# Shared norm statistics in the gated node pass, the tails' product first on TensorE, and the last layer's edgeless blocks at three in eight steps

## The chip, the cores and the metric

The kernel runs on one core of a Trainium2 chip. The metric is the device time of one execution in microseconds, where less is better. The engines of a core are PE (TensorE, its weight loads shown apart as PEld), DVE (VectorE), ACT (ScalarE), POOL (GpSimd) and SP (SyncE, which only issues DMAs here). Each runs its own instruction stream, and they meet at semaphores.

## The reference

Four graph networks follow one another over 100,000 nodes of 128 features and 50,000 edges sorted by target (`dst`); a layernorm of `x + f(x)` follows each. The first is two graph convolutions, the second a gated one with two norms, the third attention with three heads, the fourth six graph convolutions (widths 64, 32, 16, 32, 64, 128) and a last product. What matters here, cut down:

```python
def _layernorm(x, axis=-1, eps=1e-05):
    m = jnp.mean(x, axis=axis, keepdims=True)
    v = jnp.var(x, axis=axis, keepdims=True)
    return (x - m) / jnp.sqrt(v + eps)

# second network, behind the edges' messages (agg) and their batch norm
h = agg + x
mu = h.mean(axis=-1, keepdims=True); var = h.var(axis=-1, keepdims=True)
h = (h - mu) * jax.lax.rsqrt(var + EPS) * ln_gamma + ln_beta
h = jax.nn.relu(h)
return h + x                       # and then the second norm, _layernorm

# fourth network
def _gcn_conv(h, W, b, row, col, norm, n):
    h = h @ W
    msg = h[row] * norm[:, None]
    return jax.ops.segment_sum(msg, col, num_segments=n) + b
h = relu(_gcn_conv(x, W1, b1, ...)) ... h = relu(_gcn_conv(h, W6, b6, ...))
return h @ Wf + bf
```

## The kernel before

The nodes are kept in two regions. Region a has a row for each edge slot that ends a run of equal targets: 99 blocks (`NBA`) of 512 rows, 4 rows to a partition. Region b has all nodes without the edges' part: 98 blocks (`NB`) of 1024 rows, 8 rows to a partition. A pass is one `nc.Block` that ends in a barrier of all engines (`end_pass`). Inside it each engine runs a list of stages `(fn, lag, blocks)` through `pipeline`: at step t it calls, in the order of the list, each `fn` for block t - lag. So the order of a list is the order of the engine's instructions within a step, and nothing is sorted at run time. A fourth entry `every` spaces the blocks of a stage by that many steps.

**The gated node pass** (`gated_node_pass`, class `GatedNode`, tiles `cn_*`) runs the second network's node part for a and b side by side. In a step DVE does, in this order: copies of the scores, `stats_1` for a and b (`bn_stats` and `bn_aggr` on `v`), `factors_2` for a and b (minus the mean, the reciprocal of the root, their product), `shift`, `rectify`, `stats_2` for a and b (on `y`), `factors_1` for a and b. ACT does `root_2`, `normalise_1`, `root_1`, `normalise_2` and `evacuate`, each for a and then b. POOL does `gain` and `batch_norm`. Class `Norm` (L597 to L642) holds the tiles and the instructions of one norm of one region: four `Norm` objects are in use, two for a, two for b.

**The graph passes** g1 to g8 (`graph_pass`) are one convolution each. POOL gathers 4 tiles of 128 source rows per step (L1318) into one of 4 buffers; it may refill a buffer once DVE has combined the block that used it. DVE adds the rows up run by run (`add_up`, L880 and L884), in `combine`. At the last step, block 98, `join` (L896 to L902) copies the unfinished last run of each partition (`last`), waits until PE has multiplied it with `link_up` (`sum_tails`, L892), and adds the result. On PE `sum_tails` stands behind the products of that step.

With the edge part of one layer, a pass also carries layers for region b that need no edges, as `others`: tuples of a lag, `every`, the layer it follows and the layer (tiles `g_bb_*` for the first of them, `g_bc_*` for the last layer's). The last layer, the costliest (W6, Wf, bias, residual, norm), is split over g5, g6 and g7: `last_layer(0)` to `(2)` with 33, 33 and 32 blocks, one every 3 steps, from step 5 in g5 and from step 0 in g6 and g7. Within it (`deep`) PE does `turn` at lag 0, `multiply_turned` at 2 and `multiply_b` at 4; ACT `evacuate` at 1, `evacuate_b` at 3, `root` at 6, `normalise` at 8; DVE `last_rows` and `variance` at 5 and `factors` at 7. `turn` of a block waits until `evacuate_b` of the block before it has emptied the PSUM tile `p_t`.

## Time and profile before

| | us |
|---|---|
| median of 3 runs (12212.0 to 12260.14) | 12238.38 |
| profiled execution, whole | 12327.15 |
| its span | 12325.4 |
| gated node pass in it | 4090 to 5313 |
| g3, g4 | 7611 to 8319, 8319 to 8928 |
| g5 | 8928 to 9743 |
| g6 | 9743 to 10401 |
| g7 | 10401 to 11062 |
| g8 | 11062 to 12325 |

| engine | busy us | share of the span |
|---|---|---|
| PE | 6734.9 | 55% |
| DVE | 8163.0 | 66% |
| ACT | 5969.5 | 48% |
| POOL | 7335.5 | 60% |

The passes lie end to end, so a microsecond won in one is a microsecond of the whole. The shares of the whole span are means over passes with different limits; each pass has to be read for itself. The profiled execution took 0.7% longer than the median of the other runs.

### The profile page before, as it was taken

Reading aid. Unit: us, or ns where it says so; the run is one execution under the profiler, and the core shown is the slowest. Engines: PE = TensorE matmul, PEld = TensorE weight load, DVE = VectorE, ACT = ScalarE, POOL = GpSimd, SP = SyncE. Lnnn points to the kernel's source line nnn. Section 1 sums busy time; section 2 is a strip of 40 time slices with the busy share of each in tenths; the row PEclk is TensorE's granted clock in tenths of the full one; section 3 lists DMA queues with packets and bytes.
Section 4 is the critical chain, followed back from the end, with each engine's and each line's share of the span. In section 5 each row is a group of like instructions: output and inputs, shape, how many; then the busy total and the mean of one; then the engine's idle time right before and its main releaser. Section 6 shows DMA issues by size and latency. Waiting matters only on the chain. (4 is left out here: it accounts for less than half of the span.)

```text
span 12325.4 us, 143095 instructions
## 1 busy us (share of the span) xinstructions
PE 6734.9 (55%) x32436; PEld 5466.4 (44%) x32436; DVE 8163.0 (66%) x34473; ACT 5969.5 (48%) x14065; POOL 7335.5 (60%) x6801
## 2 busy tenths in 40 slices
PE   2141666665766465677746665773455565554443
PEld 1021555654555455567745665662233333332222
DVE  1063778995666899989988886444555565664444
ACT  0000445775666899989957775331123332322222
POOL 5701446886777688866636665546554455556665
PEclk6575888887888555578868887555566655665555
DMA  3238777883222577734424443443333332332221
GB/s 95 91 119 264 235 237 257 289 289 117 70 70 70 171 220 220 217 126 140 142 90 161 162 165 128 135 130 76 83 107 115 100 90 87 105 103 56 56 58 53
DMA packets 1019506, 1694.53 MB, mean 137 GB/s; under 512 B 304877, under 2 KB 535080, under 8 KB 1018594
## 3 DMA queue, kind: packets, MB, share of 16 engines
q1 hardware_dynamic: 782752, 1361.06, 33.0%
q0 software_dynamic: 175936, 218.82, 7.9%
q10 hardware_dynamic: 59970, 105.49, 2.6%
q8 instruction: 270, 4.42, 0.1%
q14 instruction: 578, 4.73, 0.1%
HBM read 988.03 MB, written 707.78 MB: 138 GB/s over the span
## 5 line engine op out<-in xcount | busy, mean ns | idle before, releaser
L1318 POOL DMA_INDIRECT g_got<-scaled,row_src x2352 | 2230.9, 949 | 1754.8 <-issue 681.8
L588 PE MATMUL g_a_p_z<-sb_L_gnn_W,g_a_u_t 128*128 128x128 f32 (+3 forms) x2574 | 665.7, 403 | 1163.7 <-ACT g_a_u_t L1163 439.5
L1163 ACT COPY g_a_u_t<-g_a_p_t 128x512 f32<-128x512 f32 (+3 forms) x495 | 226.2, 457 | 1800.4 <-remote 1223.5
L880 DVE SCALAR_TENSOR_TENSOR g_sums<-g_got,first,g_sums 128x128 f32<-128x128 f32 (+3 forms) x3136 | 869.9, 277 | 344.2 <-DMA g_got<-scaled,row_src 113.2
L588 PEld LDWEIGHTS g_a_p_z<-sb_L_gnn_W,g_a_u_t 128*128 128x128 f32 (+1 forms) x2574 | 491.6, 270 | 1342.4 <-issue 606.8
L588 PE MATMUL g_bb_p_z<-sb_L_gnn_W,g_bb_u_t 128*128 128x128 f32 (+2 forms) x4302 | 842.9, 363 | 308.9 <-DVE g_bb_z L1055 280.6
L884 DVE SCALAR_TENSOR_TENSOR g_sums<-g_sums,cont,g_got 128x128 f32<-128x128 f32 (+3 forms) x3128 | 887.6, 284 | 90.8 <-DVE g_sums L880 65.9
L1318 POOL DMA_INDIRECT g_got<-xs,idx_src x392 | 370.7, 946 | 934.5 <-POOLq L174 552.9
L588 PEld LDWEIGHTS g_bb_p_z<-sb_L_gnn_W,g_bb_u_t 128*128 128x128 f32 x4302 | 752.7, 260 | 369.9 <-ACT g_bb_u_t L1163 261.0
L1163 ACT COPY g_bb_u_t<-g_bb_p_t 128x1024 f32<-128x1024 f32 (+2 forms) x294 | 233.6, 795 | 1318.8 <-remote 555.1
L1230 POOL DMA_INDIRECT out<-g_a_o,idx_out x396 | 395.3, 998 | 361.3 <-ACT g_a_o L640 234.6
L579 PE MATMUL g_bb_p_t<-ident,g_bb_own 128*128 128x128 f32 x2151 | 365.1, 311 | 430.5 <-DMA g_bb_own<-in_x 390.2
L2383 POOL DMA_INDIRECT gb_got<-x,row_src x392 | 393.7, 1004 | 242.2 <-POOLq L174 138.3
L1475 POOL DMA_INDIRECT cg_got_src<-x,row_src x392 | 399.8, 1020 | 228.5 <-issue 101.3
L1055 DVE TENSOR_TENSOR g_bb_z<-g_bb_p_z,row_L_gnn_b 128x1024 f32<-128x1024 f32 (+1 forms) x196 | 186.6, 952 | 508.1 <-remote 383.0
L1524 PE MATMUL cg_p_g<-gate_w,cg_t_d 128*128 128x259 f32 x784 | 313.3, 488 | 380.8 <-ACT cg_t_a L1548 314.3
L579 PEld LDWEIGHTS g_bb_p_t<-ident,g_bb_own 128*128 128x128 f32 x2151 | 302.4, 168 | 461.9 <-DMA g_bb_own<-in_x 391.8
L1137 PE MATMUL g_a_p_t<-g_a_u_t,sb_L_gnn_W 64*128 64x512 f32 x198 | 200.7, 1114 | 557.9 <-ACT g_a_u_t L1163 325.8
L2507 PE MATMUL gb_p_m<-head_w,gb_u_t 128*128 128x128 f32 x2376 | 409.9, 350 | 149.8 <-DVE gb_a_r L2479 115.4
L1475 POOL DMA_INDIRECT cg_got_dst<-x,row_dst x392 | 418.7, 1068 | 119.5 <-issue 119.5
L790 PE MATMUL p_hist<-f_hot_lo,f_hot_hi 128*98 128x512 bf16 x784 | 228.4, 451 | 474.0 <-issue 414.9
L1191 ACT ACTIVATE g_bb_o<-g_bb_z 128x1024 f32<-128x1024 f32 (+3 forms) x294 | 196.6, 669 | 596.3 <-DVE g_bb_z L1055 355.3
(500 smaller groups left out, 24621.7 us busy)
## 6 DMA issues: line engine op xcount, KB each, us to landing
raw<-gb_u SPq DMA_DIRECT2D x98, 768.0 KB
xs<-f_o ACTq DMA_DIRECT2D x97, 516.0 KB
f_x<-in_x ACTq DMA_DIRECT2D x97, 512.0 KB
g_bb_own<-in_x SPq DMA_DIRECT2D x97, 512.0 KB
wide<-g_bb_o SPq DMA_DIRECT2D x97, 512.0 KB
g_bb_own<-wide SPq DMA_DIRECT2D x97, 512.0 KB
g_bb_res<-in_x SPq DMA_DIRECT2D x97, 512.0 KB
x<-g_bb_o SPq DMA_DIRECT2D x97, 512.0 KB
```

Source lines behind the costliest of these rows:

```text
L579: last = nc.tensor.transpose(dst_psum[0:n * k, q * P:q * P + p], tile[0:p, q * g * k:(q * g + n) * k], ident[0:p, 0:p])
L588: last = nc.tensor.matmul(dst_psum[0:p, q * g * width:(q * g + n) * width], turned_tile[0:n * k, q * P:q * P + p], weight[0:n * k, 0:n * w ...
L790: ins = nc.tensor.matmul(p_hist[0:HI, h * half:(h + 1) * half], hot_hi[b.s][:, (2 * c + h) * HI:(2 * c + h + 1) * HI], hot_lo[b.s][:, c * ...
L880: nc.vector.scalar_tensor_tensor(out=self.firsts, in0=new, scalar=first[:, col], in1=self.firsts, op0=ALU.mult, op1=ALU.add).then_inc(run_ ...
L884: nc.vector.scalar_tensor_tensor(out=self.part(b.s, c), in0=before, scalar=cont[:, col], in1=new, op0=ALU.mult, op1=ALU.add).then_inc(run_ ...
L1163: last = nc.scalar.copy(to, source)
L1230: nc.gpsimd.indirect_dma_start(self.to, bass.IndirectOffsetOnAxis(ap=idx_out[:, b.n * CH + c:b.n * CH + c + 1], axis=0), self.o_s[b.s4][:, ...
L1318: pool.indirect_dma_start(got[b.s4][:, c * row:(c + 1) * row], None, table, bass.IndirectOffsetOnAxis(ap=index[:, b.n * CH + c:b.n * CH + ...
L1475: pool.indirect_dma_start(got[b.s4][:, c * D:(c + 1) * D], None, x1, bass.IndirectOffsetOnAxis(ap=index[:, b.n * CH + c:b.n * CH + c + 1], ...
L1524: last = nc.tensor.matmul(p_g[c][:, :], rows, weight, start=(i == 0), stop=(i == 2))
L2383: pool.indirect_dma_start(got[b.s4][:, c * D:(c + 1) * D], None, x2, bass.IndirectOffsetOnAxis(ap=row_src[:, b.n * CH + c:b.n * CH + c + 1 ...
L2507: last = nc.tensor.matmul(p_m[:, c * D:(c + 1) * D], u_t[h][:, c * P:(c + 1) * P], head_w[:, h * D:(h + 1) * D], start=(h == 0), stop=(h = ...
```

## The change

Three things change.

1. In the gated node pass a class `BothNorms` takes the place of the four `Norm` objects: one object for each norm, with tiles 12 columns wide (4 of a, then 8 of b). The statistics still take one `bn_stats` and one `bn_aggr` for each of the 12 rows, but all 12 `bn_stats` come first and all `bn_aggr` behind them, with one wait between. Root, minus mean, reciprocal and product are one instruction each for both regions. Each such instruction waits for both regions. The scaling on ACT stays one instruction per row.
2. On PE `sum_tails` moves to the head of the list in all graph passes but g5 (`plain`).
3. The spacing of blocks becomes a pair `(steps, blocks)`: block n comes n * steps // blocks steps behind the lag. The last layer runs at (8, 3), which gives gaps of 2, 3 and 3 steps, with 32, 33 and 33 blocks in g5, g6 and g7. Its `evacuate_b` moves from lag 3 to lag 2, the step in which its input is multiplied. All others stay at one block a step.

```diff
 def pipeline(eng, stages):
-    stages = [(fn, lag, blocks, every[0] if every else 1) for fn, lag, blocks, *every in stages]
-    for t in range(max(lag + (blocks - 1) * every + 1 for _, lag, blocks, every in stages)):
-        for fn, lag, blocks, every in stages:
-            n, off = divmod(t - lag, every)
-            if off == 0 and 0 <= n < blocks:
-                fn(Block(n // UNROLL, n % UNROLL, n == blocks - 1))
+    stages = [(fn, {lag + n * every[0][0] // every[0][1] if every else lag + n: n for n in range(blocks)}, blocks)
+              for fn, lag, blocks, *every in stages]
+    for t in range(max(max(at) + 1 for _, at, _ in stages)):
+        for fn, at, blocks in stages:
+            if t in at:
+                fn(Block(at[t] // UNROLL, at[t] % UNROLL, at[t] == blocks - 1))
...
-                    return self.on(lag, every, (self.normalise, 8), (self.evacuate_b, 3), (self.root, 6), (self.evacuate, 1)), []
+                    return self.on(lag, every, (self.normalise, 8), (self.evacuate_b, 2), (self.root, 6), (self.evacuate, 1)), []
...
-                        stages = []
+                        stages = [] if plain else in_a((edges.sum_tails, 0))
...
-                        stages += in_a((edges.sum_tails, 0))
-                        if not plain:
-                            stages += in_a((na.turn, 0))
+                        stages += in_a((edges.sum_tails if plain else na.turn, 0))
...
+            class BothNorms:
...
+                def variance(self, b, tiles):
+                    stats, mv = self.stats[b.s], self.mv[b.s]
+                    self.steps.at(b)
+                    for (first, p, j), tile in zip(self.rows(b), tiles):
+                        for q in range(j):
+                            last = nc.vector.bn_stats(stats[0:p, 6 * (first + q):6 * (first + q + 1)],
+                                                      tile[0:p, q * D:(q + 1) * D])
+                    last.then_inc(self.steps.sem, 1)
+                    nc.vector.wait_ge(self.steps.sem, self.steps.count())
+                    for first, p, j in self.rows(b):
+                        for q in range(first, first + j):
+                            last = nc.vector.bn_aggr(mv[0:p, 2 * q:2 * q + 2], stats[0:p, 6 * q:6 * q + 6])
+                    last.then_inc(self.varied, 1)
...
+                def factors(self, b):
+                    self.factor_step.at(b)
+                    nc.vector.wait_ge(self.rooted, b.n + 1)
+                    nc.vector.tensor_scalar(self.minus[b.s], self.mv[b.s][:, 0:2 * self.G:2], -1.0, None, ALU.mult)
+                    nc.vector.reciprocal(self.rstd[b.s][:, :], self.sd[b.s][:, :]).then_inc(self.factor_step.sem, 1)
+                    nc.vector.wait_ge(self.factor_step.sem, self.factor_step.count())
+                    nc.vector.tensor_tensor(self.nmr[b.s][:, :], self.rstd[b.s][:, :], self.minus[b.s], ALU.mult
+                                            ).then_inc(self.factored, 1)
...
+                        def stats_1(b):
+                            dve.wait_ge(mark_a.combined, b.n + 1)
+                            dve.wait_ge(mark_b.combined, min(b.n + 1, NB))
+                            n1.variance(b, [n.v_s[b.n % 3] for n in (na, nb)])
...
+                        pipeline(dve, [(na.scores, 9, NBA), (nb.scores, 9, NB), (stats_1, 2, NBA), (factors_2, 6, NBA),
                                        (na.shift, 5, NBA), (nb.shift, 5, NB), (na.rectify, 5, NBA), (nb.rectify, 5, NB),
-                                       (na.stats_2, 5, NBA), (nb.stats_2, 5, NB), (na.factors_1, 2, NBA),
-                                       (nb.factors_1, 2, NB)])
+                                       (stats_2, 5, NBA), (factors_1, 2, NBA)])
...
+                        pipeline(act, [(n2.root, 6, NBA), (na.normalise_1, 3, NBA), (nb.normalise_1, 3, NB), (n1.root, 2, NBA),
+                                       (na.normalise_2, 6, NBA), (nb.normalise_2, 6, NB), (na.evacuate, 7, NBA),
+                                       (nb.evacuate, 7, NB)])
...
-        third = -(-NB // 3)
+        EACH, LAST = (1, 1), (8, 3)
+        thirds = [NB * part // 3 for part in range(4)]
```

**DVE in the gated node pass**, from the first statistics of a step to its second norm's factors. `cn_a_v` and `cn_b_v` are the inputs of the first norm, `mv` mean and variance, `sd` the root, `rstd` and `nmr` the factors. Before:

```order
L611 BN_STATS cn_a_n_stats<-cn_a_v 128x6 x4
L615 BN_AGGR cn_a_n_mv<-cn_a_n_stats 128x2 x4
L611 BN_STATS cn_b_n_stats<-cn_b_v 128x6 x8
L615 BN_AGGR cn_b_n_mv<-cn_b_n_stats 128x2 x8
L628 TENSOR_SCALAR cn_consts<-cn_a_n_mv 128x4
L629 RECIPROCAL cn_a_n_rstd<-cn_a_n_sd 128x4
L632 TENSOR_TENSOR cn_a_n_nmr<-cn_a_n_rstd,cn_consts 128x4
L628 TENSOR_SCALAR cn_consts<-cn_b_n_mv 128x8
L629 RECIPROCAL cn_b_n_rstd<-cn_b_n_sd 128x8
L632 TENSOR_TENSOR cn_b_n_nmr<-cn_b_n_rstd,cn_consts 128x8
```

After:

```order
L1706 BN_STATS cn_n_stats<-cn_a_v 128x6 x4
L1706 BN_STATS cn_n_stats<-cn_b_v 128x6 x8
L1712 BN_AGGR cn_n_mv<-cn_n_stats 128x2 x12
L1723 TENSOR_SCALAR cn_consts<-cn_n_mv 128x12
L1724 RECIPROCAL cn_n_rstd<-cn_n_sd 128x12
L1726 TENSOR_TENSOR cn_n_nmr<-cn_n_rstd,cn_consts 128x12
```

Six factor instructions of 4 and 8 columns become three of 12, and the eight statistics of b stand ahead of the aggregation of a.

**PE at the last host step of g3**, with the tails' product at L892 (L893 after). Before:

```order
L588 MATMUL g_a_p_z<-sb_L_gnn_W,g_a_u_t 128x64 x2
L588 MATMUL g_bb_p_z<-sb_L_gnn_W,g_bb_u_t 112x64 x3
L588 MATMUL g_bc_p_z<-sb_L_gnn_W,g_bc_u_t 128x64 x2
L579 MATMUL g_bc_p_t<-ident,g_bc_own 128x128 x2
L892 MATMUL g_sums<-g_last,link_up 128x64
L579 MATMUL g_a_p_t<-ident,g_a_z 128x128 x2
```

After:

```order
L893 MATMUL g_sums<-g_last,link_up 128x64
L589 MATMUL g_a_p_z<-sb_L_gnn_W,g_a_u_t 128x64 x2
L589 MATMUL g_bb_p_z<-sb_L_gnn_W,g_bb_u_t 112x64 x3
L589 MATMUL g_bc_p_z<-sb_L_gnn_W,g_bc_u_t 128x64 x2
L580 MATMUL g_bc_p_t<-ident,g_bc_own 128x128 x2
```

The tails' product moves ahead of the products of a, b and the second edgeless layer.

**PE in the middle of g5**, where `g_bc_p_t` is written by `turn` (64x128 x8) and by `multiply_turned` (128x512 x2), and `g_bb` is the layer with one block a step. Before:

```order
L1115 MATMUL g_bc_p_t<-ident,g_bc_own 64x128 x8
L588 MATMUL g_bb_p_z<-sb_L_gnn_W,g_bb_u_t 128x256 x2
L579 MATMUL g_bb_p_t<-ident,g_bb_own 128x128 x2
L588 MATMUL g_bc_p_z<-sb_L_gnn_Wf,g_bc_h_t 128x128 x8
L588 MATMUL g_bb_p_z<-sb_L_gnn_W,g_bb_u_t 128x256 x2
L579 MATMUL g_bb_p_t<-ident,g_bb_own 128x128 x2
L1137 MATMUL g_bc_p_t<-g_bc_u_t,sb_L_gnn_W 128x512 x2
L588 MATMUL g_bb_p_z<-sb_L_gnn_W,g_bb_u_t 128x256 x2
L579 MATMUL g_bb_p_t<-ident,g_bb_own 128x128 x2
L1115 MATMUL g_bc_p_t<-ident,g_bc_own 64x128 x8
```

After:

```order
L580 MATMUL g_bb_p_t<-ident,g_bb_own 128x128 x2
L1138 MATMUL g_bc_p_t<-g_bc_u_t,sb_L_gnn_W 128x512 x2
L1116 MATMUL g_bc_p_t<-ident,g_bc_own 64x128 x8
L589 MATMUL g_bb_p_z<-sb_L_gnn_W,g_bb_u_t 128x256 x2
L580 MATMUL g_bb_p_t<-ident,g_bb_own 128x128 x2
L589 MATMUL g_bb_p_z<-sb_L_gnn_W,g_bb_u_t 128x256 x2
L580 MATMUL g_bb_p_t<-ident,g_bb_own 128x128 x2
L589 MATMUL g_bc_p_z<-sb_L_gnn_Wf,g_bc_h_t 128x128 x8
L1138 MATMUL g_bc_p_t<-g_bc_u_t,sb_L_gnn_W 128x512 x2
```

In a gap of two steps `turn` of the next block now follows `multiply_turned` directly, where before the two were never in one step.

## Rows read from the trace of the kernel before

**Rows 1.** Busy time by stretch: us, then PE, PEld, DVE, ACT, POOL; clock, DMA, GB/s.
```profile
4090.00:5313.00 1223.00, 718.54 (x3530) 682.61 (x3530) 1159.52 (x6687) 1144.31 (x2947) 953.82 (x592) 0.53 0.70 214
8928.00:9743.00 815.00, 419.74 (x1514) 297.71 (x1514) 449.71 (x2142) 264.33 (x559) 370.75 (x392) 0.64 0.37 113
9743.00:10401.00 658.00, 390.90 (x1223) 247.77 (x1223) 397.51 (x2043) 198.41 (x462) 370.75 (x392) 0.56 0.30 86
```

**Rows 2.** Waits, 4500 to 4800 (gated node pass): total us, times, longest.
```profile
ACT cn_b_n_sd L620 <- DVE cn_b_n_mv L615: 10.5, 25, 0.7
```

**Rows 3.** DVE in order of time in that pass: start, us, line; last, one group's span.
```profile
4602.56 0.86 DVE L611 BATCH_NORM_STATS2 cn_a_n_stats<-cn_a_v 128x6 f32<-128x128 f32 x4
4603.45 0.38 DVE L615 BATCH_NORM_AGGREGATE cn_a_n_mv<-cn_a_n_stats 128x2 f32<-128x6 f32 x4
4603.75 1.61 DVE L611 BATCH_NORM_STATS2 cn_b_n_stats<-cn_b_v 128x6 f32<-128x128 f32 x8
4605.39 0.64 DVE L615 BATCH_NORM_AGGREGATE cn_b_n_mv<-cn_b_n_stats 128x2 f32<-128x6 f32 x8
4605.95 0.15 DVE L628 TENSOR_SCALAR cn_consts<-cn_a_n_mv 128x4 f32<-128x4 f32 x1
...
4606.28 0.17 DVE L628 TENSOR_SCALAR cn_consts<-cn_b_n_mv 128x8 f32<-128x8 f32 x1
...
4606.67 0.70 DVE L1794 TENSOR_TENSOR cn_a_p_h<-cn_a_y,cn_consts 128x512 f32<-128x512 f32 x1
...
4609.00 1.22 DVE L1802 SCALAR_TENSOR_TENSOR cn_b_y<-cn_b_p_h,cn_b_x_r 128x1024 f32<-128x1024 f32 x1
4610.14 0.86 DVE L611 BATCH_NORM_STATS2 cn_a_n_stats<-cn_a_y 128x6 f32<-128x128 f32 x4
...
L611 DVE BATCH_NORM_STATS2 cn_a_n_stats<-cn_a_v x396: 274/279/296, 4098.0 to 5267.3; 128x6 f32<-128x128 f32 x198
```

**Rows 4.** ACT in order of time, the same steps.
```profile
4606.25 0.28 ACT L620 ACTIVATE cn_a_n_sd<-cn_a_n_mv,eps 128x4 f32<-128x4 f32 x1
4606.44 0.29 ACT L620 ACTIVATE cn_b_n_sd<-cn_b_n_mv,eps 128x8 f32<-128x8 f32 x1
...
4612.63 0.30 ACT L620 ACTIVATE cn_a_n_sd<-cn_a_n_mv,cn_eps 128x4 f32<-128x4 f32 x1
```

**Rows 5.** Waits for the tails' product: all eight passes, then DVE in g3 and g6.
```profile
  PE g_sums L892: 22.6, 8
...
8302.13 0.22 DVE L898 COPY g_joined<-g_sums 128x64 f32<-128x64 f32 x1 [7.71 <-PE g_sums L892]
...
10377.51 0.17 DVE L898 COPY g_joined<-g_sums 128x16 f32<-128x16 f32 x1 [4.67 <-PE g_sums L892]
```

**Rows 6.** Waits of POOL in g5 (8930 to 9712), then g6 (9745 to 10377).
```profile
POOL g_got L1318 <- DVE g_sums L1015: 277.7, 30, 9.8
...
POOL g_got L1318 <- DVE g_a_own L1018: 137.2, 34, 5.7
```

**Rows 7.** DVE in g5, in order of time: a block of the last layer; the stall after.
```profile
9302.32 1.22 DVE L1067 TENSOR_TENSOR g_bc_y<-g_bc_p_z,g_bc_res 128x1024 f32<-128x1024 f32 x1
...
9307.07 0.20 DVE L880 SCALAR_TENSOR_TENSOR g_sums<-g_got,first,g_sums 128x16 f32<-128x16 f32 x1
...
9325.99 0.69 DVE L1055 TENSOR_TENSOR g_bb_z<-g_bb_p_z,row_L_gnn_b 128x512 f32<-128x512 f32 x1 [9.00 <-remote]
```

**Rows 8.** DVE at the ends of g5 and g6: last host rows, next pass.
```profile
9714.78 0.23 DVE L1091 SCALAR_TENSOR_TENSOR g_a_o<-g_sums,inv 128x64 f32<-128x64 f32 x1
...
9742.81 0.29 DVE L866 COPY g_sums<-row_L_gnn_bf 128x128 f32<-128x128 f32 x1 [7.51 <-PEq L174]
...
10385.31 0.29 DVE L1091 SCALAR_TENSOR_TENSOR g_a_o<-g_sums,inv 128x128 f32<-128x128 f32 x1
...
10401.30 0.29 DVE L866 COPY g_sums<-row_L_gnn_bf 128x128 f32<-128x128 f32 x1 [7.51 <-PEq L174]
```

**Rows 9.** PE in the tail of g5, in order of time.
```profile
9719.76 1.89 PE L1115 MATMUL g_bc_p_t<-ident,g_bc_own 128*64 128x128 f32 x8 [1.30 <-ACT g_bc_h_t L1176]
```

More of the change, by code:

```diff
@@ L1680, in gated_node_pass, with __init__ @@
             class GatedNode:
-                def __init__(self, sb, ps, r, consts, p_sc, other):
+                def __init__(self, sb, ps, r, beta, p_sc, norms, other):
                     n, G = r.name, r.per
@@ L1697, in __init__ @@
                     self.x_t = sb(f"{n}_x_t", [D, G * P])
-                    self.n1, self.n2 = Norm(sb, f"{n}_n1", r), Norm(sb, f"{n}_n2", r)
+                    (self.n1, self.n2), self.first = norms, 0 if self.a else rows_a.per
                     self.p_x = ps(f"{n}_p_x", [P, G * P])
@@ L1804, in rectify @@
                         in1=self.x_r[b.s][0:p, 0:j * D], op0=ALU.max, op1=ALU.add).then_inc(m.summed_b, 1)
-                def stats_2(self, b):
-                    nc.vector.wait_ge(self.m.summed_b, b.n + 1)
-                    self.n2.variance(self.link_c, self.y_s[b.n % 4], b, self.m.varied_b)
-                def factors_2(self, b):
-                    m = self.m
-                    self.link_g.at(b)
-                    nc.vector.wait_ge(m.rooted_b, b.n + 1)
-                    if b.after(2):
-                        nc.vector.wait_ge(m.normed_b, b.n - 1)
-                    self.n2.factors(self.link_g, b, m.factored_b, minus=self.minus[1][b.s])
                 def scores(self, b):
@@ L1851, in normalise_2 @@
                         act.wait_ge(m.turned, b.n - 1)
[L1852 removed]
+                    self.n2.scale(self.o_s[b.s], self.y_s[b.n % 4], b, self.first, p, j).then_inc(m.normed_b, 1)
                 def evacuate(self, b):
@@ L2539, in build @@
         attention_pass()
-        third = -(-NB // 3)
+        EACH, LAST = (1, 1), (8, 3)
+        thirds = [NB * part // 3 for part in range(4)]
         def last_layer(part):
-            start = part * third
-            return layer(mark_c, 64, D, scaled2[64], NA, out, w["L3_gnn_W6"], None, True, to_base=0, start=start,
-                         blocks=min(third, NB - start), residual=x3, residual_base=NA, last_w=w["L3_gnn_Wf"],
+            return layer(mark_c, 64, D, scaled2[64], NA, out, w["L3_gnn_W6"], None, True, to_base=0, start=thirds[part],
+                         blocks=thirds[part + 1] - thirds[part], residual=x3, residual_base=NA, last_w=w["L3_gnn_Wf"],
                          last_bias=brow["L3_gnn_bf"], bias_col=bcol["L3_gnn_b6"])
```

114 lines of the change are left out of this document (71 added, 43 removed).

## The prediction

> **What bounds the kernel now.** I read the stretches of the passes first, since they lie end to end. In the gated node pass DVE is busy 1160 of 1223 us and ACT 1144, while g5 takes 815 us and g6 658, both with no engine busy over 61% of them [rows 1]. So the first is bound by throughput and the graph passes by waits.
>
> In the gated node pass I then read who waits. ACT waits for DVE's last `bn_aggr` on b once a step, 10.5 us over 25 steps or 0.42 us a step [rows 2]. DVE waits for nobody: its instructions follow one another without a gap of note [rows 3]. DVE sets the step, with ACT 0.42 us behind it. The first statistics of 99 blocks start between 4098.0 and 5267.3 [rows 3]: (5267.3 - 4098.0) / 98 = 11.93 us a step.
>
> In g5 to g7 POOL gathers for 3 steps on end and then waits until DVE has freed a buffer. In g5 that wait is 277.7 us in 30 times, 9.3 us each; in g6 137.2 us in 34 times, 4.0 us each [rows 6]. During the wait DVE stands still too, for 9.00 us before 9325.99 [rows 7], until PE's products are announced to it. After that DVE does a block of the last layer, from 9302.32 to 9307.07 in the cycle before [rows 7], and only then frees a buffer. So 4.75 us of each g5 wait is the last layer's `last_rows` and `variance`, which stand ahead of `combine` in this pass; in g6 they stand behind it.
>
> **Part 1, shared norm factors and statistics: -77 us.** Per step, on DVE:
> - Factors. The three instructions of a take 4606.28 - 4605.95 = 0.33 us, those of b 4606.67 - 4606.28 = 0.39 [rows 3]. From 4 to 8 columns it grew by 0.06, so 12 columns take 0.45. The pair costs 0.72, so 0.27 goes; two norms: 0.54.
> - Statistics. Four `bn_stats` take 4603.45 - 4602.56 = 0.89, eight take 5.39 - 3.75 = 1.64; four `bn_aggr` 0.30, eight 0.56 (to 5.95) [rows 3]. On the same lines 12 take 2.39 and 0.82, 3.21 in all for 3.39 now: 0.18 for each norm, 0.36.
> - A new wait. `stats_2` of a starts at 4610.14 while `rectify` of b, from 9.00 for 1.22 us, runs until 10.22 [rows 3]. Now it waits for that end and a handoff of 0.03 (a's aggregation starts 3.45, its statistics end 3.42): 0.11 lost. `stats_1` waits for b's input as well, which POOL made a step earlier by the lags (batch norm 1, statistics 2): nothing.
> The sum is 0.54 + 0.36 - 0.11 = 0.79 us, times 98 = 77 us.
>
> ACT must follow. Its work is 11.93 - 0.42 = 11.51 us a step. It loses one root of `root_1`, 4606.44 - 4606.25 = 0.19, and one of `root_2`, 0.30 [rows 4], and comes to 11.02; DVE comes to 11.14. ACT stays just behind, so the cap of this part is (11.93 - 11.02) x 98 = 89 us. ACT's `normalise_2` of a now needs the factors of both regions; in the step shown those of b are done at 4606.67, about when ACT reaches it (4606.44 + 0.19), and the shared ones come 0.4 us earlier relative to that, so it does not wait. Behind DVE and ACT stand PE and POOL: POOL is busy 954 of 1223 us and PE 719 [rows 1], so both have slack.
>
> A rule speaks for more. That rows 3 start b's first factor 0.33 us after a's, though the three instructions last 0.15 to 0.17 us each behind one another, shows starts that overlap earlier instructions. The Trainium skill ("VectorE: DVE Perf Modes", § The DRAIN you can't avoid) says that the next DVE instruction does not start until the pipe is empty. By it each of the 6 removed instructions would give back its whole duration, about 1 us a step, and ACT's cap of 89 us would be reached. In rows 3 the rule does not hold for these short instructions, so the sum goes by the starts.
>
> **Part 2, the tails' product first: -8 us outside g5 to g7.** DVE waited 22.6 us for it in 8 passes, 7.71 of them in g3 [rows 5]. In g6 it was 4.67 [rows 5]; I put g5 (unchanged) and g7 at some 3 together, so that about 15 are in the other five. The copy of 0.17 us [rows 5], a product and the way back remain, which I put at 0.6 in each, so 12 can go. PE must still do the products that stood ahead, and edgeless layers end g3 and g4 later than the join: I take two thirds. Ends: 0 and -12.
>
> **Part 3, three blocks in eight steps: -29 us, less 8.** A pass has 99 steps. At every 3 the last of 33 blocks starts at 5 + 96 = 101 in g5 and is scaled 8 steps later, at 109; at (8, 3) the last of 32 starts at 5 + 82 = 87 and is stored by step 96. The tails go:
> - g5: from region a's last rows, 9714.78, to the next pass, 9742.81, is 28 us [rows 8]. A store and the barrier remain, some 7: -21. But 32 blocks instead of 30 now have `last_rows` inside the host steps, each for a wait of 9.3 instead of about 4.0 [rows 6]: +11. Net -10.
> - g6: 10385.31 to 10401.30 is 16.0 us, and shrinks by 9; the join wait shrinks by 4; the block that DVE does between join and last rows (4.75 as above) is gone; one block more inside costs 1 to 3. Net -15.
> - g7: the same with a shorter tail, estimated from g6's rows: the join wait, smaller there, 1.5; a block's DVE work, which in part lies beside the tail already, 4; an extra block +1.5. Net -4.
>
> **The price of the gaps of two.** There `turn` of a block stands behind `multiply_turned` of the block before, and waits for ACT's `evacuate_b` in the same step. The tail of g5 has just this sequence today: PE idles 1.30 us for it [rows 9]. It will do so at 11 places in each of three passes: 33 x 1.30 = 43 us of PE time. If POOL's gathers hide it, 0; if it is all on the path, 43. PE is idle about half of g5 and 40% of g6 [rows 1], and one place in a burst of three steps seldom decides: I take +8. The phase of the blocks against the bursts of three steps changes too, in either direction (rivals 1 and 3).
>
> **Sum.** -77 - 8 - 29 + 8 = -106 us against the profiled span of 12325.4. The execution around it adds 2 us and doesn't change; the median of the runs is 0.7% below it, and I apply the same difference to it: 12238 - 106 = **12132 us**, 0.87% less. What a measurement of this kernel can tell from no change is about 0.5%, 61 us.
>
> **Rivals.**
> 1. *The last layer comes loose from the bursts in g5.* Every 3 steps and bursts of 3 steps lock: its 4.75 us always fall between PE's announcement and the freed buffer [rows 7]. At 2, 3, 3 they drift; two thirds would fall where POOL still gathers: 32 x 4.75 x 2/3 = 101, of which some 70 remain after other waits. Against it: a late `combine` stops POOL by itself, and the burst then locks to the new place. 12062 us. Chance 0.13.
> 2. *The joined waits take back half of part 1.* If DVE finds region b's input not ready at `stats_1`, or ACT the shared factors, 0.4 us a step go: +39, 12171 us. Against it: the slack of a whole step on POOL. Chance 0.10.
> 3. *The gaps of two lie on the path, and the shifted phases cost g6 and g7 a little.* +43 for all places instead of +8, and about +15 for phases: 12182 us. Chance 0.15.
> 4. *Slower: PE stalls for a whole burst at the gaps of two.* PE's products of 9314 to 9318 reached DVE only at 9326, after 9.00 us idle [rows 7]. If the step's new round trip from PE to ACT and back meets this delay each time, `turn` waits 9 us at 33 places: +297 on the sum, 12429 us. It decides from (106 + 61) / 33 = 5 us a place for a slowdown of over 0.5%. Against it: the delay passes together for all products of a burst. Chance 0.04.
> 5. *DVE gives back whole durations* (the rule above: what the removed instructions last, 6 x about 0.16), and ACT caps it at 89: 12120 us. Chance 0.05.
> That the change does less than it says has no case: the order shows three factor instructions for six and the tail empty of the last layer.
>
> **How the numbers follow.** The forecast, 12132, has 0.53; its own range is 12090 to 12175, from the caps of part 1 (60 to 89), part 2 (0 to 12) and the gaps (0 to 43). The range for 8 in 10 leaves out rival 4, half of rival 1 and a third of rival 3: 12050 to 12205. Faster by over 0.5% means under 12177: the forecast but for 0.05, rivals 1 and 5, 0.06 of rival 2 and 0.05 of rival 3, in all 0.77. Slower by over 0.5% is rival 4: 0.04. The rest, 0.19, is within.
>
> **What would show it.** The gated node pass 77 us shorter (1146 instead of 1223), DVE still busy 94% or more of it and ACT still waiting for DVE's `bn_aggr`, now below 0.2 us a step; if POOL's v is waited for by DVE, rival 2. The waits for the tails' product down to some 5 us in all. No last-layer instruction after region a's last rows in g5 to g7, and the starts of the next passes 10, 15 and 4 us earlier against their own starts. POOL's waits in g5 at 9 us, about 32 of them; if they fall below 240 us in sum, rival 1. PE waiting for `g_bc_h_t` 1.3 us at 11 places in a pass; at 5 us or more, rival 4. Wrong altogether would be a gated node pass that keeps its 11.9 us a step.

## The result and the profile after

| | before | after |
|---|---|---|
| median of the timed runs, us | 12229.0 | 12030.7 |
| profiled execution's span, us | 12325.4 | 12030.4 |
| gated node pass | 1226.9 | 1157.6 |
| g1, g2 | 790.8, 921.8 | 777.9, 921.4 |
| g3, g4 | 707.9, 608.8 | 682.1, 599.4 |
| g5 | 815.1 | 730.6 |
| g6, g7 | 658.5, 660.9 | 611.4, 635.3 |
| g8 | 1263.3 | 1263.2 |

The changed kernel takes 0.9836 of the time before (95% interval 0.9824 to 0.9847): 198 us less, where 106 were forecast and the range ended at 12050. The two profiles lie 295 us apart, since that of before was slower than its timed runs and that of after was not. So some rows above show more than the change did. In the gated edge pass, whose code is the same, 1222.7 became 1209.7; and g3, of which the change touches only the place of the tails' product, took 682 to 720 us in the twelve profiles of this case whose whole lasts over 12000 us (the others come from chips that run every version faster, see the experiments). The median before is over four runs now, where the forecast had three and 12238. Of the runs below one, at 13940 us beside five from 10484 to 10497, was in a slower state of the chip and isn't counted.

**Gated node pass.** The windows of the trace after (us, then busy time of PE, PEld, DVE, ACT, POOL, clock, DMA share, GB/s), for the gated node pass, g5 and g6, as in [rows 1]:

```profile
4062.00:5220.00 1158.00, 715.72 (x3534) 689.76 (x3534) 1089.97 (x6106) 1101.80 (x2751) 950.49 (x592) 0.53 0.73 225
8789.00:9520.00 731.00, 378.22 (x1486) 261.35 (x1486) 446.77 (x2122) 257.25 (x548) 369.71 (x392) 0.71 0.42 124
9520.00:10131.00 611.00, 358.76 (x1223) 237.22 (x1223) 403.94 (x2043) 198.17 (x462) 369.79 (x392) 0.58 0.33 93
```

The waits of ACT and POOL in 300 us of it, as in [rows 2] (total, times, longest):

```profile
POOL cn_b_y L1824 <- ACT cn_b_y L1731: 39.3, 26, 1.8
...
ACT cn_n_sd L1717 <- DVE cn_n_mv L1712: 0.7, 2, 0.4
```

DVE in order of time in one step, as in [rows 3], and last the group of the first statistics:

```profile
4592.09 0.86 DVE L1706 BATCH_NORM_STATS2 cn_n_stats<-cn_a_v 128x6 f32<-128x128 f32 x4
4592.87 1.62 DVE L1706 BATCH_NORM_STATS2 cn_n_stats<-cn_b_v 128x6 f32<-128x128 f32 x8
4594.52 0.91 DVE L1712 BATCH_NORM_AGGREGATE cn_n_mv<-cn_n_stats 128x2 f32<-128x6 f32 x12
4595.35 0.16 DVE L1723 TENSOR_SCALAR cn_consts<-cn_n_mv 128x12 f32<-128x12 f32 x1
4595.40 0.22 DVE L1724 RECIPROCAL cn_n_rstd<-cn_n_sd 128x12 f32<-128x12 f32 x1
...
4595.73 0.69 DVE L1833 TENSOR_TENSOR cn_a_p_h<-cn_a_y,cn_consts 128x512 f32<-128x512 f32 x1
...
4598.07 1.21 DVE L1841 SCALAR_TENSOR_TENSOR cn_b_y<-cn_b_p_h,cn_b_x_r 128x1024 f32<-128x1024 f32 x1
4599.38 0.87 DVE L1706 BATCH_NORM_STATS2 cn_n_stats<-cn_a_y 128x6 f32<-128x128 f32 x4
...
4601.83 0.91 DVE L1712 BATCH_NORM_AGGREGATE cn_n_mv<-cn_n_stats 128x2 f32<-128x6 f32 x12
...
4603.40 0.86 DVE L1706 BATCH_NORM_STATS2 cn_n_stats<-cn_a_v 128x6 f32<-128x128 f32 x4
...
L1706 DVE BATCH_NORM_STATS2 cn_n_stats<-cn_a_v x396: 272/275/295, 4072.9 to 5169.8; 128x6 f32<-128x128 f32 x198
```

The step is (5169.8 - 4072.9) / 98 = 11.19 us, where it was 11.93. A statistics block takes 4595.35 - 4592.09 = 3.26 us (3.39 before), the factors 4595.73 - 4595.35 = 0.38 (0.72 for the pair). The new wait is there: `rectify` of b ends at 4598.07 + 1.21 = 4599.28, and the statistics behind it start at 4599.38. From start to start that is 1.31 us, where it was 4610.14 - 4609.00 = 1.14. ACT hardly waits for the statistics now: 0.7 us in all, where it was 10.5. In these 300 us ACT is busy 296.9 and DVE 293.1, so the two are level, and by that more taken from DVE alone would hardly shorten the step.

**Ends of the passes.** The waits for the tails' product in all eight passes, as in [rows 5], and DVE at the end of g5, as in [rows 8]:

```profile
  PE g_sums L893: 8.8, 8
...
9515.96 0.17 DVE L899 COPY g_joined<-g_sums 128x16 f32<-128x16 f32 x1 [0.70 <-PE g_sums L893]
...
9517.42 0.23 DVE L1092 SCALAR_TENSOR_TENSOR g_a_o<-g_sums,inv 128x64 f32<-128x64 f32 x1
9520.62 0.30 DVE L867 COPY g_sums<-row_L_gnn_bf 128x128 f32<-128x128 f32 x1 [2.97 <-PEq L175]
```

From region a's last output to the next pass it is now 3.2 us (9517.42 to 9520.62); it was 28. From the join (`g_joined`) to the next pass it is 4.7 us (9515.96 to 9520.62), where it was 29.5 (9713.33 to 9742.81).

**POOL in g5 and g6**, its waits for a free buffer, as in [rows 6] (total, times, longest), and then PE's greatest wait in g5:

```profile
POOL g_got L1319 <- DVE g_sums L1016: 235.0, 35, 9.6
...
POOL g_got L1319 <- DVE g_a_own L1019: 116.5, 36, 5.5
...
PE g_bc_p_t L1116 <- ACT g_bc_h_t L1177: 201.8, 20, 11.7
```

In g5 the wait is 42.7 us shorter, though PE now stands 201.8 us for ACT's `g_bc_h_t` (64.9 before), which rival 4 feared. POOL in order of time, with its idle time before each burst in brackets, shows where it is won:

```profile
9239.27 0.94 POOL L1319 DMA_INDIRECT g_got<-scaled,row_src  x1 [9.52 <-DVE g_sums L1016]
...
9248.01 0.94 POOL L1319 DMA_INDIRECT g_got<-scaled,row_src  x1 [0.30 <-issue]
9252.17 0.94 POOL L1319 DMA_INDIRECT g_got<-scaled,row_src  x1 [3.22 <-DVE g_sums L1016]
...
9265.91 0.94 POOL L1319 DMA_INDIRECT g_got<-scaled,row_src  x1 [0.30 <-issue]
9276.23 0.94 POOL L1319 DMA_INDIRECT g_got<-scaled,row_src  x1 [9.38 <-DVE g_sums L1016]
```

Each row is a gather, 1.25 us apart within a burst. From 9239.27 there are 8 of them (two steps), then 3.22 us of idle time; from 9252.17 there are 12 (three steps), then 9.38. So a gap of two steps between blocks of the last layer makes a cycle of 9252.17 - 9239.27 = 12.9 us, and a gap of three one of 24.1. Two thirds of the cycle before, 24.24 us for three steps, would be 16.2 for two: each gap of two gives back 3.3 us. The last layer's block on DVE (4.75 us) lies in another place in the two cycles: in the trace before it is wholly inside a pause of POOL for 28 of 33 blocks and behind the last gather for the other 5; in the trace after it is wholly inside a pause for 20 of 32, partly for one, and beside a burst for 11, one in three.

**What holds the pauses.** PE in g5 of the kernel before, and DVE's first row that needs its product:

```profile
9314.71 1.03 PE L588 MATMUL g_bb_p_z<-sb_L_gnn_W,g_bb_u_t 128*128 128x256 f32 x4
...
9315.58 0.38 PE L579 MATMUL g_bb_p_t<-ident,g_bb_own 128*128 128x128 f32 x2
9315.89 0.29 PEld L1137 LDWEIGHTS g_bc_p_t<-g_bc_u_t,sb_L_gnn_W 64*128 64x128 f32 x2 [0.17 <-issue]
...
9325.99 0.69 DVE L1055 TENSOR_TENSOR g_bb_z<-g_bb_p_z,row_L_gnn_b 128x512 f32<-128x512 f32 x1 [9.00 <-remote]
```

By the records PE ends the product for `g_bb_z` at 9315.74; DVE gets it at 9325.99, 2.5 us after POOL's burst, whose last gather ended at 9323.51. The ends of PE's rows are a model: the Trainium skill ("Perfetto Trace Analysis", § Tensor Engine Instruction (MATMUL, LD_WEIGHTS)) says that the profiler estimates them and that the update of the semaphore comes when PSUM acknowledges the write. So the rows don't tell whether the product itself was late or only its announcement; that it reached DVE 10.25 us behind the modelled end is measured.

The same place on a chip of another kind (see the experiments), where DVE starts 0.17 us behind PE's end while POOL gathers on:

```profile
8099.37 1.49 PE L589 MATMUL g_bb_p_z<-sb_L_gnn_W,g_bb_u_t 128*128 128x256 f32 x3
...
8100.97 0.94 POOL L1319 DMA_INDIRECT g_got<-scaled,row_src  x1 [0.30 <-issue]
8101.03 0.68 DVE L1056 TENSOR_TENSOR g_bb_z<-g_bb_p_z,row_L_gnn_b 128x512 f32<-128x512 f32 x1
...
8102.21 0.94 POOL L1319 DMA_INDIRECT g_got<-scaled,row_src  x1 [0.30 <-issue]
```

### The profile page after: what moved, and what is told of

The parts are those of the page before. It is cut to its first block and busy times, and to the rows that moved or that the text cites. A ratio compares the mean times of both kernels' runs of the same rounds, so it can differ in the third digit from the quotient of the medians.

```text
span 12030.4 us, 142319 instructions
## 1 busy us (share of the span) xinstructions
PE 6638.5 (55%) x32436; PEld 5450.5 (45%) x32436; DVE 8099.9 (67%) x33889; ACT 5912.3 (49%) x13869; POOL 7313.3 (61%) x6801
## 5 line engine op out<-in xcount | busy, mean ns | idle before, releaser
L2565 PEld LDWEIGHTS gb_p_m<-head_w,gb_u_t 128*128 128x128 f32 x2376 | 406.9, 269 | 162.8 <-issue 153.0
L694 POOL DMA_INDIRECT f_got<-in_x,idx_dst x396 | 399.9, 1010 | 128.2 <-issue 128.2
```

The lines of the kernel that those rows point to most:

```text
L694: pool.indirect_dma_start(got[b.s4][:, c * D:(c + 1) * D], None, a["x"], bass.IndirectOffsetOnAxis(ap=idx_dst[:, b.n * CH + c:b.n * CH + c ...
L2565: last = nc.tensor.matmul(p_m[:, c * D:(c + 1) * D], u_t[h][:, c * P:(c + 1) * P], head_w[:, h * D:(h + 1) * D], start=(h == 0), stop=(h = ...
```

## The experiments

The runs fell on six chips (the number of the first result's isn't recorded), of two kinds. On chips 3, 4, 11 and 15, as on the chip of the first result, the kernel before takes 12229 to 12316 us, and products that PE finishes late in a burst of POOL's gathers reach the other engines only behind the burst: I call this the hold. On chips 7 and 12 it takes 10518 and 10524, and there is no hold: in g5 of the four profiles there DVE waits 62 times for the product of `g_bb_z`, and starts 0.04 us behind PE's end each time. In g5 of the kernel before, with the hold, 30 of 31 such starts come more than 1 us behind it, at the median 9.3. Not every product is held there. Of the waits of DVE and ACT for region b's products in the bursts of 12, 31 end within 0.5 us of PE's end, all but one of them for products that PE ended in the first 6.2 us of a burst; 56 end 8.0 to 10.3 us behind it, for products ended 6.9 us or more after a burst's start. The two kinds differ in the first pass too, which has none of the changed code: PE's waits in 578 us of it, before, and then without the hold:

```profile
PE p_hist L790 <- issue: 414.9, 24, 19.1
...
PE p_hist L791 <- DVE f_hot_lo L725: 14.3, 3, 13.9
```

Every run is compared with the kernel before on its own chip.

**1. The norms alone** (without the hold, chip 12): the changed kernel with the other two parts taken back.

```diff
-                    return self.on(lag, every, (self.normalise, 8), (self.evacuate_b, 2), (self.root, 6), (self.evacuate, 1)), []
+                    return self.on(lag, every, (self.normalise, 8), (self.evacuate_b, 3), (self.root, 6), (self.evacuate, 1)), []
...
-                        stages = [] if plain else in_a((edges.sum_tails, 0))
+                        stages = []
...
-                        stages += in_a((edges.sum_tails if plain else na.turn, 0))
+                        stages += in_a((edges.sum_tails, 0))
+                        if not plain:
+                            stages += in_a((na.turn, 0))
...
-        EACH, LAST = (1, 1), (8, 3)
-        thirds = [NB * part // 3 for part in range(4)]
+        EACH, LAST = (1, 1), (3, 1)
+        thirds = [0, 33, 66, NB]
```

> Only the shared statistics and factors of the gated node pass; all else is as in the kernel before. If the gated node pass of the changed kernel (1157.6 us, before 1226.9) owes its time to this part alone, the pass takes 1157 us again and the whole is 65 to 75 us faster than the kernel before (ratio about 0.994), with g5 at 815 us, g6 at 658 and g7 at 661. Rival: the profile of before was slow by chance in this pass too, and the part alone is worth under 50 us in the timed runs.

0.9934 (0.9921 to 0.9946), 72 us; the gated node pass 1155.0 us. The pass owes its time to this part, and it is as long with the hold, where it was 1154 to 1158 us in all profiles with this code. The expected times of g5 to g7 were missed, since this chip has no hold: 529.9, 522.6 and 511.9 us.

**2 and 3. The tails' product alone** (chip 12, then chip 4 with the hold). The edit is the kernel before with `sum_tails` at the head of PE's list.

> Only the tails' product at the head of PE's list in all graph passes but g5. Theory A, the part acts at the join alone: waits for the product fall from 22.6 to about 9 us, g3 is some 7 us shorter than 708, the whole 8 to 13 us faster. Theory B, the 20 us by which the gathers of g3 ran shorter in the changed kernel belong to it: g3 takes 682 us here too, and the whole is 35 us or more faster.

> The tails' product first, alone, again. With the hold: 10 to 20 us, since in the first two traces its waits fell by 14 us; the 20 us of g3's gathers are chance, because g3 alone varied between 682 and 720 us in five profiles with the same work. Rival: it is worth over 30 us there. Without the hold: 9 us as before.

Without the hold 0.9990 (0.9981 to 0.9999), 9 us. With it 0.9997 (0.9986 to 1.0009): nothing that can be told from zero. The 10 to 20 us that I expected there did not come, though the waits for the product fell from 22.6 us to some 9. g3 took 704.4 us, so the short g3 of the first profile is not this part's work (it is 682.4 on chip 11 as well, and 695.7 to 720.1 on the others with the hold). What the waits gave up is in part paid back by the products that now stand behind: from the join to the next pass g3 went from 16.8 to 18.3 us.

**4 and 5. The spacing alone** (chip 12, then chip 4). The edit is the kernel before with `(8, 3)`, the new thirds and `evacuate_b` at lag 2.

> Only the last layer at three blocks in eight steps, with its second evacuation a step earlier; gated node pass and tails' product as before. Theory A, the gain of g5 is the spacing of the blocks: POOL's gathers come in bursts of 12 behind a gap of three steps (cycle 24.1 us) and of 8 behind a gap of two (12.6 us), g5 takes 730 us, g6 about 616, g7 about 638, the whole 125 to 150 us faster in the profile. In the timed runs, whose sum was 198, what is left after norms (70) and tails (10) is about 120. Theory B, part of it belongs to the other edits: g5 stays above 760 us.

> The last layer's spacing alone, again, for a chip that holds PE's announcements while POOL gathers (the kernel before takes about 12250 us there). With the hold: the whole 198 less the norms' 72 and the tails' 9 are its own, 110 to 125 us (ratio about 0.9905), of which g5's gathers are 30 to 45, g6's and g7's 35 or less, the tails of the passes 49, the join waits behind a burst 25. If it gives under 60 us, the parts help each other and the sum of them taken alone is short of the whole. Without the hold: 36 us as before.

Without the hold 0.9965 (0.9952 to 0.9978), 36 us, far from the 120 of theory A, which was made for bursts and pauses that this chip doesn't have; with it 0.9909 (0.9888 to 0.9929), 105 us by the medians and 112 by the ratio, as expected. POOL's waits for a buffer in g5, by the spacing of three without the hold (norms alone), by the new spacing without it, and by the new spacing with it:

```profile
POOL g_got L1319 <- DVE g_sums L1016: 0.3, 1, 0.3
...
POOL g_got L1319 <- DVE g_sums L1016: 23.3, 20, 2.1
...
POOL g_got L1319 <- DVE g_sums L1016: 242.1, 35, 9.7
```

Without the hold POOL hardly waits, and the gaps of two cost: the gathers of g5 take 505.8 us from first to last instead of 488.1. With the hold they gain: 720.1 instead of 755.8 (chip 4, tails' product alone).

**6. The changed kernel again** (chip 3, with the hold).

> The changed kernel once more, unaltered. If this chip holds PE's announcements while POOL gathers (the kernel before then takes about 12230 us), it repeats the first result: ratio 0.984, g5 at 730 us. If it doesn't (the kernel before takes about 10520 us), the parts measured apart add up: 72 + 9 + 36 = 117 us, a ratio of 0.989, with g5 at 522 us and g6 at 501. A sum over 135 or under 100 would say that the parts act on each other.

0.9847 (0.9827 to 0.9867), 180 us. The parts alone come to 72 + 1 + 105 to 112 = 178 to 185 (the 72 from a chip without the hold): they add up. Its passes lie between those of the two first profiles: g5 744.6, g6 638.2, g7 640.6. Without the hold the whole was not run; the parts alone sum to 117.

**7. g5 at every three steps, 30 blocks** (chip 3).

```diff
-        thirds = [NB * part // 3 for part in range(4)]
+        thirds = [0, 30, 64, NB]
...
-                           (5, LAST, mark_b, last_layer(0))))
+                           (5, (3, 1), mark_b, last_layer(0))))
```

> The changed kernel with g5's blocks at every three steps again, 30 of them so that none stands in the tail, and 34 each in g6 and g7. Theory A (a gap of two steps costs where gathers are bound by nothing else, and gains where announcements are held): without the hold g5's gathers take 488 us instead of the 506 of the spacing of eight, and the kernel is 10 to 18 us faster than the changed one; with the hold they take about 757 - 10 instead of 713, and it is about 35 us slower. Theory B (the spacing of the blocks doesn't matter, only where they end): within 5 us of the changed kernel on either chip.

0.9899 (0.9874 to 0.9924), 49 us slower than the changed kernel on the same chip, and g5 is 49 us longer: 793.7 us against 744.6. Its gathers take 756.8 us, as before the change, against 726.7. The last gather to the join takes 26.6 against 12.6, since the pass ends on a burst of three steps. So the spacing itself is worth some 30 us in the gathers, which the forecast left out of its sum. The earlier `evacuate_b` is in this kernel too, so by itself it gives g5 nothing; whether the gaps of two need it was not run.

**8. The wait for ACT at every block** (chip 3, one run).

```diff
-                    return self.on(lag, every, (self.multiply_b, 4), (self.multiply_turned, 2), (self.turn, 0))
+                    return self.on(lag, every, (self.multiply_b, 4), (self.multiply_turned, 3), (self.turn, 0))
...
-                    return self.on(lag, every, (self.normalise, 8), (self.evacuate_b, 2), (self.root, 6), (self.evacuate, 1)), []
+                    return self.on(lag, every, (self.normalise, 8), (self.evacuate_b, 3), (self.root, 6), (self.evacuate, 1)), []
...
-        EACH, LAST = (1, 1), (8, 3)
-        thirds = [NB * part // 3 for part in range(4)]
+        EACH, LAST = (1, 1), (3, 1)
+        thirds = [0, 33, 66, NB]
```

> The changed kernel with the last layer at every three steps in all three passes (33, 33, 32 blocks) and its first product and second evacuation at lag 3, so that the next block's transposes stand right behind the product and wait for ACT at every block. Theory A, this wait itself is what costs: without the hold g5's gathers take over 500 us, 1 us or more for each of 30 blocks above 488; with the hold bursts are cut as behind a gap of two (8 gathers and fewer). Theory B, the wait is hidden and only the two steps' distance is short: without the hold 488 us; with it bursts of 12 and cycles of 24.1 us.

POOL's waits in g5, then in g6:

```profile
POOL g_got L1319 <- DVE g_sums L1016: 277.1, 31, 9.7
...
POOL g_got L1319 <- DVE g_a_own L1019: 289.9, 32, 10.2
```

In g5 nothing changed: 277.1 us, bursts of 12, as theory B had it. But PE waited for ACT only 42.1 us here, 32 times, 1.3 us each, and not the 10 us that it waits at the gaps of two. So the run shows that a short wait at every block doesn't cut a burst; what a long one would do behind a gap of three it doesn't tell. In g6 POOL's waits went from 137.2 to 289.9 us, the pass took 822.6 us where it was 658.5, and g7 went from 661 to 742; the one execution took 12490 us, 182 more than the kernel before. In g6 DVE's last rows now wait 209.0 us for their product (108.4 before), which reaches them in the pause, 17.1 us after the burst's start. Of the two moves in this kernel it isn't told apart which does it.

**9 and 10. g5 at every two steps** (chip 7 without the hold, chip 4 with it).

```diff
-                           (5, LAST, mark_b, last_layer(0))))
+                           (5, (2, 1), mark_b, last_layer(0))))
```

> The changed kernel with the last layer's 32 blocks in g5 one every two steps, from step 5 to 67, and none behind. Where PE's announcements are held during POOL's gathers, as in the first two traces, theory A (a gap of two steps cuts the burst to 8 gathers, and its last rows lie beside the burst) expects cycles of 12.6 us for two steps up to step 70 and about 24 us for four steps behind it: g5 at about 640 us instead of 730.6. Theory B (the 4.7 us of every block lie on the path, wherever they are) expects no less than 730. Where nothing is held, as in the three runs before this one, g5 is bound by the gathers and stays at 515 to 530 us by both.

> The changed kernel with g5's 32 blocks one every two steps, again. With the hold, theory A (a gap of two steps gives bursts of 8 gathers and 12.6 to 13.0 us for two steps, whatever stands beside it): 32 such cycles, then four steps in about 24 us: g5 at 620 to 650 us instead of 731 to 745, the whole 90 to 110 us faster than the changed kernel. Theory B (the cheap short cycle was paid for by the two long ones around it, 24.1 us each): nothing below 720. Without the hold: 600 us against 522, as before.

Without the hold g5 takes 599.6 us, where 515 to 530 were expected, and the kernel 10486 beside 10518 (one run each). With it g5 takes 658.2, and the kernel 12050, 0.9788 (0.9768 to 0.9807), by the ratios 73 us less than the changed kernel; g5 at 620 to 650 and 90 to 110 us were expected. POOL's waits in g5, first without the hold, then with it:

```profile
POOL g_got L1319 <- DVE g_sums L1016: 107.7, 29, 7.8
...
POOL g_got L1319 <- DVE g_sums L1016: 163.8, 42, 14.2
```

With the hold the cycles are 12.6 to 16.0 us, most of them 13 to 14, so theory A holds, and its price of 12.6 to 13.0 was a little low. Without it two steps take over 12 us as well, against 10 that the gathers need: 64 steps cost 100 us. The short cycle is nearly the same on both kinds of chip. It gains only where the alternative is worse. On chip 4 the short bursts leave most of the hold behind them, too: only 3 of DVE's 29 waits for the product of `g_bb_z` end more than 1 us behind PE's end.

**11. One buffer less for POOL** (chip 4).

```diff
-                                pool.wait_ge(mark_a.combined, b.n - UNROLL + 1)
+                                pool.wait_ge(mark_a.combined, b.n - UNROLL + 1 + (tag in ("g5", "g6", "g7")))
```

> The changed kernel, in which POOL may gather only three steps ahead of DVE's combine instead of four in g5, g6 and g7. With the hold, theory A (each pause costs the same whatever the burst before it, because PE's products are announced only 2.4 us after it ends): bursts of 8, three pauses where there were two, 150 us or more slower. Theory B (PE needs little time to catch up behind a short burst): within 30 us of the changed kernel. Without the hold: g6 and g7 unchanged at 502 us, g5 10 us or less slower.

12136 us, 0.9858 (0.9836 to 0.9880), the same as the changed kernel (0.9847 on chip 3). g5 took 742.9 us, and the bursts stayed at 12 and 8: theory B. So the fourth buffer doesn't set the length of a burst.

**12. g5 at two blocks in five steps** (chip 11).

```diff
-                           (5, LAST, mark_b, last_layer(0))))
+                           (5, (5, 2), mark_b, last_layer(0))))
```

> The changed kernel with g5's 32 blocks at two in five steps, gaps of two and three in turn. Theory A (every gap of three steps is a cycle of 24.2 us, every gap of two one of 12.9 to 13.5, with the hold): 37.1 to 37.7 us for five steps, 7.5 a step, over 78 steps, where the spacing of eight has 61.4 / 8 = 7.7: g5's gathers come to 700 to 715 us against 727, and the kernel is 12 to 25 us faster than the changed one, between it and the spacing of two. Theory B (the two-step cycles stay short only behind two long ones): no faster than 727. Without the hold each gap of two costs 1.6 us, as 11 of them cost 17.7 us at the spacing of eight: 16 to 18 gaps, gathers of 514 to 517 us, g5 about 9 us longer than at the spacing of eight.

0.9820 (0.9804 to 0.9836). Its profile, on a chip where the unchanged passes took what they did in the first profile of after (g4 599.3 us beside 599.4, g8 1263.3 beside 1263.2), is 21 us shorter, g5 699.1 against 730.6, its gathers 681.1 against 712.8, a little more than expected. The cycles were 24.1 and 12.4 us in turn. Theory A holds for the cycles; that the whole kernel is faster than the changed one rests on the profiles, since the intervals of the two ratios overlap.

**13 and 14. The last layer's rows behind combine in g5** (chip 15, with the hold), at the spacing of eight and, with the two lines of experiment 7 besides, at every three steps.

```diff
-                            stages += others_of + in_a((na.combine, 0), (na.rows, 0), (na.out_rows, 0))
+                            stages += others_of[:-3] + in_a((na.combine, 0), (na.rows, 0), (na.out_rows, 0)) + others_of[-3:]
```

> The changed kernel with the last layer's rows, variance and factors behind combine in g5's DVE order, as in g6 and g7, instead of ahead of it. With the hold: theory A (the block's 4.75 us ahead of combine lengthen each pause) expects pauses of 4.7 us instead of 9.5 behind bursts of 12, g5's gathers at 610 to 640 us instead of 713 to 727, the kernel 80 to 100 us faster than the changed one. Theory B (the pause is PE's catching up, whatever DVE does first) keeps pauses of 9 us and over 700. Without the hold: the gathers stay near 500 us.

> The same with g5's 30 blocks at every three steps (34 each in g6 and g7). Theory A: with the block behind combine the spacing no longer matters, g5's gathers are within 12 us of those of the run beside it, where the order before gave 757 against 727. Theory B: 25 us or more apart, since the bursts of 8 remain cheaper. Without the hold: 488 us.

POOL's waits in g5, at (8, 3) and then at every three:

```profile
POOL g_got L1319 <- DVE g_sums L1016: 167.4, 41, 9.5
...
POOL g_got L1319 <- DVE g_sums L1016: 168.0, 54, 6.0
```

167.4 and 168.0 us, where it was 248.8 and 276.5 on chip 3. The gathers take 646.6 and 641.5 us: 5 apart where the old place had them 30 apart (on chip 3, where the kernel before takes 8 us less than on chip 15). So the place of the block is what makes the spacing count. With it ahead of combine, its time lies in POOL's pause behind a gap of three and beside the burst behind a gap of two; once it delays no buffer, the spacing doesn't matter to the gathers. The kernel at the spacing of eight takes 0.9789 (0.9764 to 0.9815), 255 us less than before and, by the ratios, about 70 less than the changed kernel, where theory A had 80 to 100; at every three steps it takes 0.9802 (0.9778 to 0.9825). By the ratios it and the kernel with g5 at every two steps (0.9788) are the fastest ones found. It was run with the hold only.

## Why the prediction was wrong

**Part 1, 77 us forecast, 72 measured.** The steps held: three factor instructions 0.38 us where I had 0.45, statistics 3.26 where I had 3.21, the new wait a loss of 1.31 - 1.14 = 0.17 us where I had 0.11, ACT's waits at 0.7 us in 300 us (some 27 steps) where I had "below 0.2" a step. Rival 2 did not show (in 300 us DVE has no wait for POOL's v), and neither did rival 5: 0.74 us a step went, not a whole microsecond, and against the rule quoted there the first factor of 4595.35 and the next of 4595.40 (`reciprocal`) start 0.05 us apart though the first lasts 0.16. The same section of the Trainium skill ("VectorE: DVE Perf Modes", § The DRAIN you can't avoid) goes on that a next instruction which is not held starts earlier; the forecast quoted it without that, and these rows agree with the exception.

**Part 2, 8 us forecast.** The waits fell by 13.8 us, from 22.6 to 8.8, in the changed kernel, and almost as far with this part alone. The time fell by 9 us without the hold and by nothing that can be told from zero with it. Within the bounds.

**Part 3, the tails.** g5's end was 21 us by the forecast and 25 in the profile (join to next pass 29.5 to 4.7). In g6 the join to the next pass went from 23.8 to 6.6 us, and the last gather to the join from 18.0 to 10.6 on chip 3; the pass became 13 to 20 us shorter on chips 4 and 3, where -15 was forecast. In g7 the same two went from 15.1 to 7.9 and from 16.5 to 12.0, and the pass became some 20 us shorter where -4 was forecast: this term was too small too.

**Part 3, the gathers: the step that failed.** The forecast put +11 in g5 ("32 blocks instead of 30 now have `last_rows` inside the host steps, each for a wait of 9.3 instead of about 4.0") and +8 for the gaps of two. The first took the wait of 9.3 us as the price of a block, whatever its distance; the second counted only what PE's 1.30 us of idle time could cost at a gap of two, and the sum had no term for what such a gap gives back. The runs show the wait of 9.3 us as the price of a gap of three steps with the last rows ahead of combine; a gap of two has 3. With some 11 of them the gathers of g5 became 30 to 36 us shorter on chips 3 and 4 (45 in the first profile), and the stretch from the last gather to the join another 14 to 15. That second stretch the forecast had left out of g5's tail. So g5 gained 71 to 78 us instead of 10, and that is the greater part of what the forecast lacks: the whole of part 3 was -21 by the forecast and is -105 to -112 alone (experiment 5).

Rival 1 named this ("The last layer comes loose from the bursts in g5") with its sign in the profile, POOL's waits below 240 us, and they are 235.0. I gave it 0.13 and 12062 us. The sign was met by 5 us only, and on chips 3 and 4 the waits are 248.8 and 242.1. Its size was off as well: I let blocks drift at two thirds of the places. They don't drift. The bursts follow the blocks, so one block in three (11 of 32) comes to lie beside the burst. The argument against it, that the burst locks to the new place, was true of the two long gaps only.

Rival 4's mechanism happened, and g5 became shorter with it: `turn` waited about 10 us at 20 places (201.8 us). In the trace PE's wait lies inside POOL's burst, where DVE and ACT stand still for PE's earlier products anyway; no run made this wait alone. The line drawn there, a slowdown from 5 us a place, was wrong: a stall counts by what it delays, not by its length. Without a hold the gaps do cost, 17.7 us in g5's gathers and nothing in those of g6 and g7 (488.1 us each, as without the gaps), within the 0 to 43 that I gave.

The forecast's own range has an error in its sum: from its caps (part 1 89 to 60, part 2 12 to 0, gaps 0 to 43) around 12132 it comes to 12108 to 12192, not 12090 to 12175. What was measured lies below either.

**What stays open.** g6's gathers were 21 us shorter in the first profile, but 620 to 627 us on chips 3 and 4 against 616 to 618 before: no gain there that repeats. g7's gathers fell by 8 to 26 us, with a spread as great as the gain, and no run takes its cause apart. The place of the block and its spacing were varied together only in g5. And why PE's products are held on one kind of chip is not settled: the runs show that in g5 it goes with POOL's longer bursts of gathers, and that the two kinds of chip differ in a pass that the change doesn't touch as well.

## What to carry to other kernels

Before the price of a stage's wait is multiplied by its count, look at what decides that wait. Here it was the distance to the next block together with the block's place in DVE's order. The trace before had almost only cycles of three steps in g5, so the price of a shorter one could not be read from it and had to be bounded. Work on a consumer that stands ahead of what frees a producer's buffer lies in the producer's pause: moving it behind, a matter of the order in one list, gave about 70 us on top of the 180 to 198 of the whole edit. When two chips run the same kernel 15% apart, a tuning found on one is to be tried on the other: against the spacing of eight, the one by two steps gave some 73 us on the one kind and cost 77 in g5 on the other (599.6 against 522.7).

## What the runs showed of the hardware

On four of the six numbered chips, and on that of the first result, DVE got PE's products late in g5: at the pauses of 9 us behind bursts of 12 gathers it started 2.2 to 3.1 us after POOL's last gather ended, mostly 2.3 to 2.6, and up to 10.3 us after PE's end in the records (kernels before and changed). In the kernel before this befell the products that PE ended 6.9 us or more after a burst's start, while those ended in the first 6.2 us came at once; with g5 at every two steps, in bursts of 8, few were late. Where the line lies is not general: with the block behind combine (chip 15) products ended 4 us after a burst's start were late too. On chips 7 and 12 DVE started 0.04 us after PE's end, beside the same gathers at the same 1.25 us each. The kernel before takes 12229 to 12316 us on the one kind and 10518 to 10524 on the other, and g5, by the same code, 815 and 530 us; that the hold is the whole of this difference is not shown. The mean granted clock of TensorE was 0.66 to 0.68 on the one kind and 0.70 to 0.71 on the other; in the first pass, where PE waits hundreds of microseconds on the one kind and 14.3 on the other, a clock that differs by a twentieth is no explanation.
